# Routed experts: all experts for every row, or rows sorted by expert through device memory

## What is computed

```python
logits = einsum('bsh,eh->bse', x, classifier_w)          # 12 routes: 8 experts, 4 that do nothing
probs = softmax(logits)
_, idx = top_k(probs + e_score_correction_bias, 2)
rw = take_along_axis(probs, idx) * 1.5
w_full = sum(one_hot(idx, 12) * rw)
act = silu(x @ gate_w[e]) * (x @ up_w[e])                # gate, up: 128 x 256 for each expert
expert_out = act @ down_w[e]                             # down: 256 x 128
out = sum over e < 8 of w_full[e] * expert_out[e]
out = out + x * sum(w_full[8:])
```

## Time and profile before

| | |
|---|---|
| median of three runs | 837.51 us (834.66 to 838.67) |
| profiled execution, first to last instruction (its span; no other time of its own is listed) | 832.7 us |
| granted TensorE clock, mean over the span | 0.986 of full |
| busy, share of the span | PE 90%, PEld 64%, DVE 74%, ACT 49%, POOL 69% |
| moved by transfers | 24.12 MB in 8,763 packets |

### The profile page before, as it was taken

One profiled execution on the slowest core, in us unless ns is written; L12 is line 12 of the kernel. 1 busy time (PEld: TensorE's weight loads), 2 busy tenths in 40 slices (PEclk: granted clock), 3 DMA queues, 4 the chain that ended last, 5 costly groups with the idle time before them and its releaser, 6 DMA issues. The chain is left out here.

```text
span 832.7 us, 14911 instructions
## 1 busy us (share of the span) xinstructions
PE 750.6 (90%) x4808; PEld 535.8 (64%) x4808; DVE 615.8 (74%) x1115; ACT 406.6 (49%) x1084; POOL 570.9 (69%) x589
## 2 busy tenths in 40 slices
PE   4999999859999999689999999999999999866785
PEld 2555555447878877556777777777777777543454
DVE  5898999868887878665565576886678667749995
ACT  1688888533322322216454544555454445444453
POOL 5667776326676757564657778787878887716976
PEclk9999999989999999999999999999999999998999
DMA  9200000040000010122110000000000000000011
GB/s 262 103 1 0 0 0 1 2 168 20 20 19 20 19 57 0 57 95 96 48 49 1 1 1 1 3 1 1 1 1 2 1 2 1 1 2 7 25 33 38
DMA packets 8763, 24.12 MB, mean 29 GB/s; under 512 B 1711, under 2 KB 5167, under 8 KB 8087
## 3 DMA queue, kind: packets, MB, share of 16 engines
q1 hardware_dynamic: 8154, 23.28, 8.5%
q10 hardware_dynamic: 549, 0.08, 0.1%
HBM read 21.26 MB, written 2.10 MB: 28 GB/s over the span
## 5 line engine op out<-in xcount | busy, mean ns | idle before, releaser
L1606 POOL TENSOR_TENSOR q<-turned 64x512 f32<-64x512 f32 x128 | 168.0, 1313 | 23.5 <-DVE turned L1532 9.5
L1283 PE MATMUL ps<-l_yt,a 128*128 128x512 f32 x576 | 144.1, 400 | 2.1 <-ACT p L1429 1.6
L1283 PEld LDWEIGHTS ps<-l_yt,a 128*128 128x128 f32 x576 | 104.9, 188 | 26.9 <-issue 4.7
L1593 POOL TENSOR_TENSOR p<-p,l_inverse 128x512 f32<-128x512 f32 x64 | 66.8, 1047 | 77.3 <-DVE l_inverse L1554 76.9
L1429 ACT ACTIVATE p<-ps,l_negmax 128x128 f32<-128x128 f32 x256 | 91.1, 382 | 43.1 <-DVE l_negmax L1523 43.1
L1532 DVE TENSOR_TENSOR turned<-ps,rope 128x1024 f32<-128x1024 f32 x64 | 78.0, 1220 | 42.4 <-PE ps L1283 39.8
L871 PE MATMUL ps<-yt_experts,wsplit 128*128 (+1 forms) x384 | 97.3, 403 | 5.7 <-DVE h L974 5.2
L467 DVE TENSOR_REDUCE negmax<-ps 128x4 f32<-128x512 f32 x128 | 84.4, 685 | 13.3 <-PE ps L290 12.8
L871 PEld LDWEIGHTS ps<-yt_experts,wsplit 128*128 128x128 f32 x384 | 71.2, 192 | 23.1 <-issue 5.4
L1523 DVE TENSOR_REDUCE l_negmax<-ps 128x4 f32<-128x512 f32 x64 | 41.2, 686 | 45.8 <-PE ps L1341 45.6
L383 ACT ACTIVATE pt<-ps 128x512 f32<-128x512 f32 x128 | 71.2, 599 | 6.8 <-PE ps L312 4.5
(11 more groups left out here) (213 smaller groups left out, 1571.1 us busy)
## 6 DMA issues: line engine op xcount, KB each, us to landing
wide<-in_wide SPq DMA_DIRECT2D x8, 768.0 KB, 4.5
mx_raw<-in_mx SPq DMA_DIRECT2D x8, 384.0 KB, 3.1
x<-in_x SPq DMA_DIRECT2D x4, 512.0 KB, 8.4
ctx_t<-in_ctx_t SPq DMA_DIRECT2D x1, 2048.0 KB, 7.8
out<-x SPq DMA_DIRECT2D x16, 128.0 KB, 1.7
narrow<-in_narrow SPq DMA_DIRECT2D x8, 192.0 KB, 2.7
ktraw<-in_ctx_rows SPq DMA_DIRECT2D x1, 1248.0 KB
wraw<-in_gate SPq DMA_DIRECT2D x1, 1024.0 KB, 18.1
```

Of the source, the lines that this page charges most:

```text
L1283: out = pe.matmul(tile_bank(n, k), a[i][:, pa, kin, k * 128:(k + 1) * 128], yt[j % 2][:, py, kin, :, :].rearrange("p b s -> p (b s)"), sta ...
L1593: pool.tensor_tensor(p[:, head, :, :], p[:, head, :, :], spread(inverse[:, head, :], 2, S), ALU.mult).then_inc(normed[head], 1)
L1606: t = pool.tensor_tensor(out[rows[(head + half) % 2], head, :], turned[rows[head], half, :], turned[rows[head], 2 + half, :], ALU.add)
```

## The change

Each row goes only to its own experts. The rows are sorted by expert into 40 blocks of 128 slots in a new tensor `slots` in device memory, every expert's rows beginning at a block of their own, so that a block has one owner.

- *Load stage.* GpSimd writes a blank row; behind its loads SP issues nine stores of it over `slots` and over a second tensor `outs`, which will hold one result for each row and choice. The semaphores of the attention are taken without a scope and cleared by GpSimd at the start of `routed_experts`. Gate and up of an expert now lie side by side. The normalised rows stay in SBUF as `m.rows`, with two more columns: where the result goes, and the route's weight.
- *Routing.* After the two masks, VectorE makes the weights and the idle share; TensorE counts the rows ahead of each row with 17 small products; VectorE makes each expert's first block, each row's slot, and each block's owner.
- *Scatters.* GpSimd issues 16 indirect scatters for the first choice, one for each sequence. When they have landed VectorE rewrites the two columns, and 16 more go out for the second choice. SP then loads `slots`, two blocks for each of 20 steps, into a ring of six buffers.
- *Blocks.* TensorE reads two owners into registers, turns the rows, multiplies them by gate and up (12 products of 256 columns), turns the gated product and multiplies it by down (6 of 256). The steps of four blocks' pairs overlap. ScalarE scales by the route's weight, and GpSimd scatters the results to `outs`, 128 rows at a time.
- *End.* When all have landed SP loads `outs` in four groups, and VectorE adds both results of each row to x and takes the statistics.
- *Side jobs.* The two multiplications of quantising move from GpSimd to VectorE; ten of 16 chunks are quantised beside the scatters, six beside the blocks. The rotation is spread over the steps. GpSimd's work on `h` and x is gone, and so are the spreading product and the zeroed tables of `turn_rows`.

The core of the diff:

```diff
+BLOCK, ROW = 128, E + 2
+BLOCKS = 2 * B + EXPERTS
 ...
+            sp.wait_ge(m.blank_made, 2)
+            for k in range(5):
+                sp.dma_start(m.slots[8 * k * BLOCK:8 * (k + 1) * BLOCK, :].rearrange("(b p) e -> p b e", p=BLOCK),
+                             spread(m.blank[:, :], 1, 8)).then_inc(m.blanked, 16)
+            for k in range(4):
+                sp.dma_start(m.outs[8 * k * S:8 * (k + 1) * S, :].rearrange("(b p) e -> p b e", p=S),
+                             spread(m.blank[:, 0:E], 1, 8)).then_inc(m.blanked, 16)
 ...
+        STEPS, RING, EARLY = BLOCKS // 2, 6, 10
 ...
+        nc.clear_and_free_semaphores(m.spent)
 ...
+            def take(i):
+                if i >= RING:
+                    sp.wait_ge(sent[(i - RING) % 4], 32 * ((i - RING) // 4 + 1))
+                sp.dma_start(taken[i % RING][:, :, :], m.slots[2 * BLOCK * i:2 * BLOCK * (i + 1), :]
+                             .rearrange("(b p) e -> p b e", p=BLOCK)).then_inc(taken_loaded[i % RING], 16)
+            def bring(j):
+                wait(sp, x_made, 2 * (j - 1))
+                for k in range(2):
+                    sp.dma_start(back[2 * (j % 2) + k], m.outs[k * B * S + 4 * j * S:k * B * S + 4 * (j + 1) * S, :]
+                                 .rearrange("(b p) e -> p b e", p=S)).then_inc(back_loaded[j % 2], 16)
 ...
+            sp.wait_ge(first_sent, 16 * B)
+            sp.wait_ge(second_sent, 16 * B)
+            for i in range(STEPS):
+                take(i)
 ...
+            for i in range(STEPS + 3):
+                if inside(i, STEPS):
+                    owners[i] = [pe.value_load(r.owner[0:1, 2 * i + b:2 * i + b + 1], min_val=0, max_val=EXPERTS - 1) for b in range(2)]
+                turn(i)
+                widen(i - 1, owners.get(i - 1))
+                turn_inner(i - 2)
+                narrow(i - 3, owners.get(i - 3))
 ...
+            for b in range(B):
+                add_idle(b)
+            for c in range(EARLY):
+                if c == EARLY // 2:
+                    dve.wait_ge(first_sent, 16 * B)
+                    dve.tensor_copy(m.rows[:, :, E].bitcast(U32), r.place[:, 1, :]).then_inc(second_made, 1)
+                    dve.tensor_copy(m.rows[:, :, E + 1], r.weight[:, 1, :]).then_inc(second_made, 1)
+                for part in range(3):
+                    quantise(c, part)
+            for i in range(STEPS + 3):
+                split_rows(i)
+                combine(i - 1)
+                split_inner(i - 2)
 ...
+            def send(k, b, done):
+                pool.indirect_dma_start(out=m.slots, out_offset=bass.IndirectOffsetOnAxis(ap=r.slot[:, k, b:b + 1], axis=0),
+                                        in_=m.rows[:, b, :], in_offset=None, bounds_check=SLOTS - 1,
+                                        oob_is_err=False).then_inc(done, 16)
+            def give(i):
+                if inside(i, STEPS):
+                    pool.wait_ge(out_kept, i + 1)
+                    for b in range(2):
+                        pool.indirect_dma_start(
+                            out=m.outs, out_offset=bass.IndirectOffsetOnAxis(ap=taken[i % RING][:, b, E:E + 1].bitcast(U32), axis=0),
+                            in_=kept[i % 4][:, b, :], in_offset=None, bounds_check=2 * B * S - 1,
+                            oob_is_err=False).then_inc(sent[i % 4], 16)
+            pool.wait_ge(m.blanked, 16 * 9)
+            pool.wait_ge(route, ROUTE_STEPS)
```

More of the change, by code:

```diff
@@ L850, in _ @@
+            for j in range(GROUPS):
+                bring(j)
         @block.tensor
         def _(pe):
[L852 to L861 removed]
@@ new lines, in turn @@
+            def turn(i):
+                if inside(i, STEPS):
+                    pe.wait_ge(taken_loaded[i % RING], 16 * (i // RING + 1))
+                    wait(pe, y_lo, i - 1)
+                    for b in range(2):
+                        for half in range(HALVES):
+                            c = (b * HALVES + half) * 128
+                            t = pe.transpose(turned_ps[i % 2][:, c:c + 128], taken[i % RING][:, b, half * 128:(half + 1) * 128],
+                                             m.ident[:, :])
+                    t.then_inc(y_turned, 1)
@@ new lines, in turn_inner, with narrow @@
+            def turn_inner(i):
+                if inside(i, STEPS):
+                    pe.wait_ge(h_made, i + 1)
+                    wait(pe, h_lo, i)
+                    for b in range(2):
+                        t = pe.transpose(inner_ps[:, b * 128:(b + 1) * 128], h[i % 2][:, b, :], m.ident[:, :])
+                    t.then_inc(h_turned, 1)
+            def narrow(i, owners):
+                if inside(i, STEPS):
+                    pe.wait_ge(h_lo, i + 1)
+                    wait(pe, out_kept, i)
+                    for b in range(2):
+                        for q, (ph, pw) in enumerate(PRODUCTS):
+                            t = pe.matmul(out_ps[:, b, :], ht[i % 2][:, ph, b * 128:(b + 1) * 128],
+                                          weight[:, pw, 2, bass.ds(owners[b], 1), :].rearrange("p x n -> p (x n)"),
+                                          start=(q == 0), stop=(q == 2))
+                    t.then_inc(out_made, 1)
@@ L910, in _, with turn_weights @@
+            def turn_weights(c):
+                pe.wait_ge(mx_made, c + 1)
+                wait(pe, mx_kept, c)
+                for k in range(3):
+                    t = pe.transpose(mx_ps[:, k * 128:(k + 1) * 128], quantised[c % 2][:, k * 128:(k + 1) * 128], m.ident16[:, :])
+                t.then_inc(mx_turned, 1)
             for b in range(B):
@@ L944, in _ @@
             act.wait_ge(centred, 1)
             act.activation(r.e[:, :, :], r.biased[:, :, :], ACT.Exp).then_inc(exp_made, 1)
-            steps(act, step)
+            for c in range(EARLY - 2):
+                keep_weights(c)
+            for i in range(STEPS + 4):
+                keep_out(i - 4)
+                keep_rows(i)
+                gate(i - 1)
+                keep_inner(i - 2)
+                if i < 2:
+                    keep_weights(EARLY - 2 + i)
+                c, part = mx_late(i - 1)
+                if part == 2:
+                    keep_weights(c)
@@ L1036, in _ @@
             choose_routes(dve, m, r, then)
-            dve.wait_ge(m.w_zero, 1)
-            for rows in (0, LO):
-                then(dve.tensor_copy(weights[:, :, rows:rows + EXPERTS], r.e[:, :, 0:EXPERTS]))
-            then(dve.tensor_reduce(r.total[:, :], r.e[:, :, EXPERTS:], AX.X, ALU.add))
-            assert count[0] == ROUTE_STEPS
-            steps(dve, step)
+            dve.tensor_tensor(r.chosen[:, :, :], r.first[:, :, 0:EXPERTS], r.second[:, :, 0:EXPERTS], ALU.add).then_inc(chosen_made, 1)
```

540 lines of the change are left out of this document (273 added, 267 removed).

## The result

The changed kernel takes **900.2 us** (median of four executions; three took 898.1 to 900.4 us, and one of 2,323 us is left out of the ratio), the kernel before 837.5 in the same session: ratio 1.0745, interval 1.0714 to 1.0776. Slower, as forecast, but by 7.5% instead of 2.4%, and outside the range of 820 to 897. The profiled execution took 900.39 us, its span 898.6, 65.9 more than before.

What follows compares the result with a forecast made beforehand. TensorE was taken to bound the routed experts. Sorting, 20 steps of 4.4 us and collecting end that stage 18.2 us later, plus 2.3 ahead: span 853.2, plus 4.8 from span to median, forecast 858 us; range 820 to 897.

Steps and rivals of the forecast that it cites:

- load stage: Start of kernel: nine more stores issued by SP at 0.45 us each, +2.0 us, and clearing semaphores 0.3.
- Rival 4: Load stage: SP can't queue nine stores behind the loads, so its barrier waits some 17 us; 875 us, chance 0.06.
- second numbers: Sorting: VectorE's rewriting of two columns for the second choice, after idle rows and five chunks; second scatters forecast from 217.3 us.
- Scatter: Sorting and blocks: GpSimd's time for one indirect scatter of 128 rows, put at 1.40 us; bounds 0.45 and 2.30.
- rival 1: Scatters are cheap, near SP's 0.45 us issue: 829 us, or 820 with owner reads hidden; chance 0.24.
- rival 2: Scatters are dear: each of the first 32 waits out a VectorE operation, 2.0 us each; 871 to 890 us, chance 0.22.
- VectorE's second five chunks lie beside this and cost nothing: Before the blocks: VectorE's 24 us of further quantising was to overlap the second scatters and first load, adding 0.
- Blocks: Twenty steps of two blocks, 4.4 us each; close bounds TensorE 3.8, GpSimd 4.06, ring of six row buffers 4.25.
- owner reads: Blocks: TensorE's two register reads of block owners, 0.6 us shown per step; bounds nothing and 3.4.
- rival 3: Half clock: TensorE at its 1.2 GHz level in the blocks, 5.6 us a step, +24 us, 882 us; chance 0.06.
- End: After the last output scatters: landing 2.0 us, then collecting four groups, statistics and barrier, 24.0 us.
- only move: Stages after the routed experts: same code and data, so merely shifted in time, 0 us change.

Runs made afterwards that it cites:

- experiment 1: Changed kernel with all nine zeroing stores moved unchanged from SP's list in the load stage to one in the attention; 864.3 us, ratio 1.0319.
- Experiment 2: As experiment 1, but two of the nine zeroing stores stay in the load stage; 880.7 us.
- experiment 4: As experiment 1, with SP's load of raw weights that waits for VectorE's tenth chunk put behind the first four loads of sorted rows; 854.7 us, ratio 1.0208.
- experiment 3: As experiment 1, with eight row buffers instead of six; 855.0 us, ratio 1.0211.
- experiment 10: experiment 9's kernel with twelve of GpSimd's twenty rotation pieces moved from the steps into its wait for the first outputs; 834.1 us, ratio 0.9973.
- experiment 11: experiment 10's kernel with TensorE reading the first step's owners once for all steps, so blocks meet wrong weights; 831.3 us, ratio 0.9930.
- experiment 5: As experiment 1, with nine chunks before the blocks, second numbers after four, idle additions singly between pieces of chunks; 851.4 us, ratio 1.0150.
- experiment 8: experiment 3's kernel with TensorE turning the identity matrix through all the collecting, up to the meeting of the engines; 852.7 us, ratio 1.0182.
- experiment 9: Changed kernel with all repairs found: experiments 1, 3, 5, 8, plus idle additions behind blocks, second numbers in halves, early statistics of twelve sequences; 837.0 us, ratio 0.999.
- experiment 6: As experiment 1, with TensorE turning the identity matrix some 200 times while rows are collected; 859.0 us, ratio 1.0263.

## Why the prediction was wrong, and where it was right

**The step that failed** is the load stage: "nine more at 0.45 us take SP to 10.4 us: +2.0 us". The price of an issue came from a row in which SP's queue had room; past that room an issue lasted as long as the queue took to drain, 18.8 us and then 3.2 each. It measured +40.0, and experiment 1, which moves nothing but the stores, lets the attention begin 39.5 us sooner. The same paragraph held the cover that mattered, "the stores themselves (9.5 MB) run beside the attention", but on the chip the attention waited for the last store's place in the queue. Rival 4 named the mechanism with a chance of 0.06 and sized it by the loads alone, 17 us. Experiment 2 shows that this is the price of two stores; nine also drain 7 x 3.2 us of themselves. Rival 4 with that drain, plus the forecast for the stage, gives afterwards 837.5 + 17 + 22 + 18 = 895, within 1% of the result.

**The stage of the experts** came out at +19.2 for +18.2, but by errors that cancel, which is luck. On the axis of before (39.2 us less): owners 186.9 (forecast 186.4), second numbers 219.0 (217.3; a chunk took 5.1 for 4.8, though the prediction's own terms add up to 4.9), last scatter 240.6 (239.7), first rows turned 252.7 (**245.1**), last scatter of outputs 341.7 (341.4), next stage 368.4 (367.4).
- *Scatter*: 1.27 with the gap, for 1.40. Right in kind; rivals 1 and 2 fall.
- *The missed wait*: "VectorE's second five chunks lie beside this and cost nothing" failed. They lie on SP's order, since a load that waits for the tenth chunk stands ahead of the takes, and on VectorE's, since the first split stands behind that chunk: 7.6 us late. With the load behind four takes (experiment 4) the rows are turned 7.7 us sooner, but split only 5.7 sooner, behind the tenth chunk.
- *Blocks*: 3.89 for 4.4. The ring paced them, as the sum had it, but only just: eight buffers take 0.1 to 0.2 off a step (experiment 3), and then GpSimd is next, at 3.73 to 3.80 for the forecast 4.06 (experiments 3 and 10). The owner reads show 0.25 to 0.36 a step up to VectorE's bound, for 0.6 (experiment 11). TensorE ran at 0.97 of its clock through the blocks, so rival 3 falls for this run; in experiments 1 and 5 the clock fell there for 14 and 17 us.
- *End*: 26.7 us from the last scatter to the next stage, for 26; paced by VectorE, four groups of 4.0 us.

**Later stages**: "only move" was wrong by 7.5. The 31 us in which TensorE is idle ahead of them cost 3.3 to 3.6 in the first 140 us through the clock (experiment 8); the other 4 lie where the granted clock was lower than before the change (0.98 for 0.99, then 0.93 for 0.96 in the last stage), for a reason that stays open. The half clock had been thought of for the blocks, not for what follows them.

**The range**, 820 to 897, did not follow from its own terms: owner reads at their upper bound give 858 + 44 = 902. That this would have held the result would have been luck: the reads showed some 5 us, not 44.

**The rule of the Trainium skill**, "SBUF — State Buffer", section "SBUF: two separate sides", that GpSimd cannot write its descriptors while VectorE holds the shared ports, agrees with one scatter in 32: 5.86 us, ending 0.9 us after sixteen additions with two operands in SBUF; with single additions between other passes the longest was 1.32 (experiment 5). The section's sentence on descriptors names VectorE's 2-port modes; that these additions ran in one no run shows. It did not cost what rival 2 took for it: the other 31 scatters, most of them beside chunk passes, took 0.97 to 1.24. Why the chunk passes held none is not shown; the prediction's guess was that descriptors slip into VectorE's gaps. The long one cost the end nothing: the first half had landed by 254, and VectorE wrote the second numbers at 258.

## What to carry to other kernels

An issue on SP's queue was cheap here only while the queue had room (0.43 us, then 18.8). Before stores are put at the end of a stage with a barrier, add up what is already queued there and ask how long it takes to drain; put them into a stage in which the queue's engine has nothing else to do.

When work is cut by half, the steps that stay in a row decide: sorting and collecting here cost as much as the products saved, and after seven repairs the kernel stood where it had begun (experiment 9). For each load in an in-order queue, look for one ahead of it that waits for a slow engine. And before a difference between two traces is put down to an edit, compare the granted clock of the stretch: 6.6 us between two traces of the same blocks went with it here.

## What was not expected of the hardware

- SP took one 1 MB store of 1,032-byte pieces in 0.43 us behind eleven loads; the next issue lasted 18.8 us, and then one store went in every 3.2 us, the rate at which they were moved (they landed 3.1 us apart).
- After 31 us without work TensorE came out of its next 140 us 3.3 to 3.6 us late. In experiment 6 it had nothing to do for only the last 5.4 us before the stage, and the granted clock still fell (0.64 over four us, then 0.51).
- The same blocks, with six row buffers, took 3.82 to 3.92 us a step in four executions, and 4.24 and 4.37 in two in which the granted clock fell to its 1.2 GHz level on the way; with eight buffers 3.73 to 3.77.
